# One kernel for two attention blocks: every engine's order and all PSUM banks dealt out anew

## The chip, the cores and the metric

The kernel runs on one core of a Trainium2 chip (trn2). The metric is the device time of one execution in microseconds, as the median of the runs shown. Engines are named as in the profile: PE (TensorE, matrix products), PEld (its weight loads), DVE (VectorE), ACT (ScalarE), POOL (GpSimd) and SP (SyncE, which here issues the DMAs).

## The reference, cut to what matters

The input is `x` and a context, both 64 sequences of 128 tokens with 256 features. Two layers follow one another.

```python
# layer 0: 16 heads of 64, keys and values from the context
qn, kn, vn = _ln(q), _ln(k), _ln(v)
attn = einsum('bhte,bhse->bhts', qn @ Wq, kn @ Wk) + rel_bias[idx]
out  = softmax(attn / 8) @ (vn @ Wv)
x    = q + out @ fc_w.T + fc_b
x    = x + gelu(_ln(x) @ W1.T + b1) @ W2.T + b2
# layer 1: 16 query heads of 16, one key/value head, a window of 128
scores = where(keep, (x @ Wq + bq) @ (ctx @ Wk + bk).T / 4, NEG)
attn = softmax(scores) @ (ctx @ Wv + bv) @ Wo + bo
gate = silu(concat([attn, x]) @ Wg + bg)
out  = attn * gate + x * (1 - gate)
y    = rms(out) * rms_w ; y = y - mean(y, axis=1)
```

## The kernel before, in words

Two sequences make a group `g`, so there are NG = 32 groups. The program of each engine is a straight list of calls that was written out by hand: a prologue, a loop `for r in range(3, NG - 3)` with 26 rounds, and an epilogue. In round `r` the attention of layer 0 for group `r` (with some of its fourth quarter from `r - 1`), the MLP of group `r - 1` and layer 1 of group `r - 2` run woven into each other. One round of the loop is called a pass here. Engines meet through counting semaphores: `till.wait_ge(name, count)` before a call, `.then_inc` at its end. The order in each list is the order of execution on that engine.

The attention of layer 0 goes in quarters `Q` of four heads: `proj_q`, `proj_k`, `proj_v` (dense products, three fp32r matmuls for one fp32 product), then `scores(g, Q)`, then `pv(g, Q)` (probabilities times V), then `fc` and `fc_lo`. Between `scores` and `pv`, DVE takes each of the two score banks with `min0` (bias and row minimum), ACT does `exps0`, DVE `inv0`, POOL `norm0`, DVE `turn0` (a transpose), and a DMA, `spread0`, lays it out. Layer 1 has `scores1(g, b)` and `pv1(g, b, n)` with `min1`, `exps1`, `inv1`, `norm1`, `turn1`, `spread1` in the same roles. `q_out` (ACT) and `k_out` (DVE) copy a projection out of PSUM into the single buffers `qT` and `kT`, so they wait until the scores of the quarter before are done, and the next scores wait for them.

Five kinds of product use a part of the PE array, that is, they are tiled: `scores` 64 rows by 128 columns (64\*128, line 757), `pv` 128\*64 (line 770), `scores1` 32\*128 (line 882), `pv1` and the small `kv_v` 128\*32 (lines 895 and 669). All others use 128\*128 and are called dense here. Two or four tiled matmuls that follow each other run on different parts of the array at once.

Every product writes one of eight PSUM banks; the tuple behind the bank in a call (`("min1", 8 * r - 7)`) is the copy that has to be done before the bank is written again. Before, banks 0 to 3 and 4 to 7 turn as two rings of four: `ring0[(r + i) % 4]`, `ring4[(r + i) % 4]`.

On ACT, `gelu` needs another table of functions than `exps0` and `exps1`; each change between them costs an `ACT_TABLE_LOAD`. Before, a pass runs both halves of `gelu` with no exponential between them.

## Time and profile before

| | us |
|---|---|
| three runs | 1902.6, 1903.36, 1907.44 |
| median | 1903.36 |
| profiled execution, span | 1903.7 |
| PE busy | 1840.5 (97% of the span) |
| PEld, DVE, ACT, POOL busy | 1696.0, 1518.9, 1538.4, 1294.2 |
| from one pass to the next | 56.74 |

The span is the profiled execution's own time from its first to its last instruction; it lies 0.3 us from the median of the runs. The page of the profile gives the busy time of each engine and the costliest groups of instructions; the time line gives instructions in order with their start; "..." stands where rows are left out. Matmuls are pipelined: one that is 0.28 us long starts 0.12 us after the one before it, so a start-to-start distance, not a duration, is what a matmul costs PE.

### The profile page before, as it was taken

Reading aid. Unit: us, or ns where it says so; the run is one execution under the profiler, and the core shown is the slowest. Engines: PE = TensorE matmul, PEld = TensorE weight load, DVE = VectorE, ACT = ScalarE, POOL = GpSimd, SP = SyncE. Lnnn points to the kernel's source line nnn. Section 1 sums busy time; section 2 is a strip of 40 time slices with the busy share of each in tenths; the row PEclk is TensorE's granted clock in tenths of the full one; section 3 lists DMA queues with packets and bytes.
Section 4 is the critical chain, followed back from the end, with each engine's and each line's share of the span. In section 5 each row is a group of like instructions: output and inputs, shape, how many; then the busy total and the mean of one; then the engine's idle time right before and its main releaser. Section 6 shows DMA issues by size and latency. Waiting matters only on the chain.

```text
span 1903.7 us, 55010 instructions
## 1 busy us (share of the span) xinstructions
PE 1840.5 (97%) x18660; PEld 1696.0 (89%) x18660; DVE 1518.9 (80%) x6787; ACT 1538.4 (81%) x5586; POOL 1294.2 (68%) x1328
## 2 busy tenths in 40 slices
...
GB/s 208 131 84 116 111 119 111 115 110 115 107 118 120 115 107 114 104 123 121 116 99 121 101 125 118 114 102 118 111 118 118 110 107 113 112 116 114 88 83 56
DMA packets 215273, 214.49 MB, mean 113 GB/s; under 512 B 29904, under 2 KB 197456, under 8 KB 214992
## 3 DMA queue, kind: packets, MB, share of 16 engines
...
q14 instruction: 133, 1.09, 0.2%
...
## 4 chain that ended last, share of the span: by engine, by line
PE 94%; DMA 2%; DVE 1%; ACT 1%; POOL 1%; issue 1%; SPq 0%; ACTq 0%; DVEq 0%; POOLq 0%
PE bank L576 12%; PE bank L577 11%; PE bank L578 11%; PE bank L594 8%; PE bank L590 8%; PE bank L591 8%; PE bank L757 7%; PE bank L770 7%; PE bank L582 4%; PE bank L882 4%; PE bank L895 3%; PE bank L583 3%; PE bank L586 3%; PE bank L654 2%; PE bank L600 2%
## 5 line engine op out<-in xcount | busy, mean ns | idle before, releaser
L2574 ACT ACTIVATE soft<-soft,row_min 128x128 f32<-128x128 f32 x1024 | 397.4, 393 | 16.3 <-DVE row_min L1728 16.0
L2494 ACT ACTIVATE soft<-soft,row_min 128x128 f32<-128x128 f32 x1024 | 397.8, 394 | 9.5 <-DVE row_min L1620 9.1
L235 DVE STREAM_TRANSPOSE turned<-soft 128x512 f32<-128x512 f32 x512 | 349.2, 692 | 9.7 <-POOL soft L3032 4.9
L3032 POOL TENSOR_TENSOR soft<-soft,inv_sum 128x512 f32<-128x512 f32 x256 | 267.1, 1044 | 127.3 <-DVE inv_sum L1628 123.3
L3041 POOL TENSOR_TENSOR soft<-soft,inv_sum 128x512 f32<-128x512 f32 x256 | 264.9, 1045 | 93.0 <-DVE inv_sum L1737 93.0
L1620 DVE CUSTOM_DVE_ANT_0 soft<-bank,relb 128x128 f32<-128x128 f32 x1024 | 231.6, 284 | 64.9 <-PE bank L757 64.5
L1728 DVE CUSTOM_DVE_ANT_0 soft<-bank,winb 128x128 f32<-128x128 f32 x1024 | 226.6, 284 | 16.9 <-PE bank L882 14.5
L2494 ACT ACTIVATION_READ_ACCUMULATOR soft<-soft,row_min 128x1 f32 x1024 | 196.7, 192 | 0.0
L2574 ACT ACTIVATION_READ_ACCUMULATOR soft<-soft,row_min 128x1 f32 x1024 | 195.1, 191 | 0.0
L1691 DVE TENSOR_TENSOR hidS<-hid,hidS 128x1024 fp32r<-128x1024 f32 x64 | 120.5, 1883 | 71.5 <-ACT hidS L2545 68.6
L757 PE MATMUL bank<-kT,qT 64*128 64x128 f32 x2048 | 148.7, 285 | 1.5 <-DVE kT L1600 1.4
L576 PE MATMUL bank<-wv,cT 128*128 128x256 f32 x512 | 147.2, 288 | 0.0
L770 PE MATMUL bank<-soft,V 128*64 128x128 f32 x2048 | 140.1, 279 | 3.7 <-issue 2.1
L577 PE MATMUL bank<-wv,cT 128*128 128x256 f32 x512 | 143.3, 280 | 0.0
L578 PE MATMUL bank<-wv,cT 128*128 128x256 f32 x512 | 143.1, 280 | 0.0
L757 PEld LDWEIGHTS bank<-kT,qT 64*128 64x128 f32 x2048 | 124.4, 187 | 20.7 <-issue 7.5
L1600 DVE TENSOR_SCALAR kT<-bank,bk 128x256 f32<-128x256 f32 x256 | 110.0, 471 | 39.7 <-PE bank L586 35.9
L770 PEld LDWEIGHTS bank<-soft,V 128*64 128x64 f32 x2048 | 109.4, 136 | 22.2 <-issue 5.7
L2526 ACT ACTIVATE hid<-bank,cols 128x256 f32<-128x256 f32 x256 | 106.2, 472 | 27.6 <-DVE hidS L1691 24.0
L590 PE MATMUL bank<-wfc,OT 128*128 128x256 f32 x512 | 127.8, 283 | 0.7 <-ACT OT L2505 0.6
L590 PE MATMUL bank<-w,hidS 128*128 128x256 f32 x512 | 123.5, 281 | 2.8 <-ACT hidS L2545 2.8
L591 PE MATMUL bank<-wfc,OT 128*128 128x256 f32 x512 | 126.0, 280 | 0.0
...
## 6 DMA issues: line engine op xcount, KB each, us to landing
soft<-turned SPq DMA_DIRECT2D x1024, 128.0 KB, 2.8
...
```

The source lines that it names most:

```text
L235: return eng.transpose(turned[:, slot, :, s % 2, :, :].rearrange("p j h b -> p h j b"), soft[:, s, :, :].rearrange("p h (j a) -> p h j a", ...
L576: pe.matmul(out, stat(LO), mov(HI), start=first, stop=False, **kw)
L577: pe.matmul(out, stat(HI), mov(LO), start=False, stop=False, **kw)
L578: return pe.matmul(out, stat(HI), mov(HI), start=False, stop=last, **kw)
L590: pe.matmul(out, stat(HI), mov(LO), start=first, stop=False, skip_group_check=True)
L591: return pe.matmul(out, stat(HI), mov(HI), start=False, stop=False, skip_group_check=True)
L757: last = pe.matmul(bank[i][:, h * SEQ:(h + 1) * SEQ], qT[half, c, b * SEQ:(b + 1) * SEQ], kT[half, c, b * SEQ:(b + 1) * SEQ], start=True, ...
L770: last = pe.matmul(bank[row:row + HS, col:col + SEQ], V[:, b, c * P + row:c * P + row + HS], pair_of_slots(Q % 2)[:, :, slot, h, :], start ...
L2494: last = act.activation(soft[:, s, h, :], soft[:, s, h, :], ACT.Exp, bias=row_min[:, s, h:h + 1], scale=-1.0, accum_out=row_sum[:, s, h:h ...
L2574: last = act.activation(soft[:, s, h, :], soft[:, s, h, :], ACT.Exp, bias=row_min[:, s, h:h + 1], scale=-1.0, accum_out=row_sum[:, s, h:h ...
L3032: pool.tensor_tensor(soft[:, m % NS0, :, :], soft[:, m % NS0, :, :], inv_sum[:, m % NS0, :].unsqueeze(2).broadcast_to([P, QUAD, SEQ]), ALU ...
L3041: pool.tensor_tensor(soft[:, s, :, :], soft[:, s, :, :], inv_sum[:, s, :].unsqueeze(2).broadcast_to([P, QUAD, SEQ]), ALU.mult).then_inc(se ...
```

## The change

No instruction's shape and no buffer changes. All five lists are in a new order, and the banks turn as two rings of three and one of two. In PE's loop, tiled products of both layers stand side by side in four stretches per pass, where there were eight. Inside the loop `proj_k`, `proj_q` and `scores` of the next group's first quarters are drawn forward, so that `scores(r + 1, 0)`, `pv(r, 3)` and `scores(r + 1, 1)` of the next round touch. On ACT, `exps0(r, 5)` now stands between the two halves of `gelu`. At the start, the DMAs of the weights and of `raw_x`, `raw_c` are issued in another order, and `cols_in` (which the first products and ACT's first weights wait for) comes seventh, not second.

PE's loop, tiled products and what stands next to them:

```diff
-        ring0 = banks[0:4]
-        ring4 = banks[4:8]
+        ring_a = [banks[i] for i in (0, 3, 6)]
+        ring_b = [banks[i] for i in (1, 5, 7)]
+        ring_c = [banks[i] for i in (2, 4)]
...
             for r in range(3, NG - 3):
...
-                scores(r, 0, (ring0[r % 4], ring4[r % 4]), (("v_out", 4 * r),), (("min1", 8 * r - 13),))
-                fc_lo(r - 1, 2, ring0[(r + 2) % 4])
...
-                scores(r, 1, (ring0[r % 4], ring4[r % 4]), (("min0", 8 * r + 1),), (("min0", 8 * r + 2),))
-                kv_k(r, ring4[(r + 2) % 4], ("q_out", 4 * r + 2))
...
-                pv1(r - 2, 0, 0, ring0[(r + 3) % 4], ("o_lo", 4 * r))
-                pv1(r - 2, 0, 1, ring0[(r + 3) % 4])
-                kv_v(r, ring4[(r + 2) % 4])
-                scores1(r - 2, 1, (ring4[r % 4], ring0[r % 4], ring0[(r + 1) % 4], ring4[(r + 3) % 4]), (("min0",
-                    8 * r + 4),), (("y_out", 2 * r - 4),), (("q_out", 4 * r + 3),), (("k_out", 4 * r + 3),))
-                out_mm(r - 2, 0, ring0[(r + 2) % 4], ("x1", r))
-                pv(r, 0, ring4[r % 4], ("min1", 8 * r - 11))
-                out_mm_lo(r - 2, 0, ring0[(r + 2) % 4])
...
-                scores(r, 2, (ring0[r % 4], ring0[(r + 1) % 4]), (("min1", 8 * r - 10),), (("min1", 8 * r - 9),))
-                turn_h(r - 1, ring0[(r + 3) % 4], ("v_out", 4 * r + 2))
...
-                pv(r, 1, ring0[r % 4], ("k_out", 4 * r + 4))
-                mlp_in(r - 1, 3, ring0[(r + 2) % 4], ("hid_out", 4 * r - 3))
...
-                scores(r, 3, (ring4[(r + 3) % 4], ring4[(r + 1) % 4]), (("q_out", 4 * r + 4),), (("hid_out",
-                    4 * r - 1),))
-                pv1(r - 2, 1, 0, ring0[(r + 2) % 4], ("hid_out", 4 * r))
-                pv1(r - 2, 1, 1, ring0[(r + 2) % 4])
-                proj_q(r + 1, 0, ring0[(r + 1) % 4], ("v_out", 4 * r + 3))
...
-                pv(r, 2, ring0[(r + 2) % 4], ("o1_lo", 2 * r - 2))
-                scores1(r - 1, 0, (ring4[(r + 3) % 4], ring0[r % 4], ring4[(r + 1) % 4], ring4[r % 4]), (("x2_lo",
-                    r),), (("o_lo", 4 * r + 2),), (("ag", 2 * r - 2),), (("q1_out", r),))
-                proj_v(r, 3, ring0[(r + 1) % 4], ("q_out", 4 * r + 5))
-                fc(r, 1, ring0[(r + 3) % 4])
-                proj_k(r + 1, 0, ring4[(r + 3) % 4], ("min1", 8 * r - 7))
...
-                pv(r, 3, ring0[r % 4], ("min1", 8 * r - 6))
...
+                scores(r, 1, (ring_c[r % 2], ring_b[(r + 1) % 3]), (("o_lo", 4 * r - 1),), (("q_out", 4 * r + 2),))
+                proj_v(r, 0, ring_b[(r + 2) % 3], ("k_out", 4 * r + 2))
...
+                center_out(r - 3, 1, ring_b[(r + 2) % 3], ("v_out", 4 * r + 1))
+                scores1(r - 2, 1, (ring_b[(r + 1) % 3], ring_c[(r + 1) % 2], ring_a[r % 3], ring_c[r % 2]), (("min0",
+                    8 * r + 4),), (("o_lo", 4 * r),), (("q_out", 4 * r + 3),), (("k_out", 4 * r + 3),))
+                pv1(r - 2, 0, 0, ring_b[r % 3], ("x1", r))
+                pv1(r - 2, 0, 1, ring_b[r % 3])
+                kv_v(r, ring_a[(r + 2) % 3])
+                pv(r, 0, ring_b[(r + 2) % 3], ("y_out", 2 * r - 4))
+                scores(r, 2, (ring_b[(r + 1) % 3], ring_b[r % 3]), (("min1", 8 * r - 11),), (("o1_lo", 2 * r - 3),))
+                out_mm(r - 2, 0, ring_c[(r + 1) % 2], ("min1", 8 * r - 10))
+                out_mm_lo(r - 2, 0, ring_c[(r + 1) % 2])
+                turn_h(r - 1, ring_b[(r + 1) % 3], ("min0", 8 * r + 5))
+                proj_k(r, 3, ring_a[r % 3], ("min1", 8 * r - 9))
+                proj_v(r, 1, ring_c[(r + 1) % 2], ("ag", 2 * r - 3))
+                mlp_in(r - 1, 0, ring_c[r % 2], ("min1", 8 * r - 8))
+                mlp_in_lo(r - 1, ring_c[r % 2])
+                mlp_in(r - 1, 1, ring_b[(r + 1) % 3], ("h_lo", r))
+                proj_q(r, 3, ring_a[(r + 1) % 3], ("kv_turn", r))
+                mlp_in(r - 1, 2, ring_c[r % 2], ("hid_out", 4 * r - 3))
+                proj_v(r, 2, ring_a[r % 3], ("k_out", 4 * r + 4))
+                fc(r, 0, ring_b[(r + 1) % 3], ("hid_out", 4 * r - 2))
+                mlp_out(r - 1, 0, 0, ring_c[(r + 1) % 2], ("v_out", 4 * r + 2))
...
+                scores(r, 3, (ring_b[(r + 2) % 3], ring_a[(r + 1) % 3]), (("o_lo", 4 * r + 1),), (("q_out",
+                    4 * r + 4),))
+                pv(r, 1, ring_c[r % 2], ("hid_out", 4 * r - 1))
+                pv1(r - 2, 1, 0, ring_b[r % 3], ("hid_out", 4 * r))
+                pv1(r - 2, 1, 1, ring_b[r % 3])
+                mlp_out_lo(r - 1, 0, 1, ring_c[(r + 1) % 2])
...
+                proj_v(r, 3, ring_c[r % 2], ("o_lo", 4 * r + 2))
+                proj_q1(r - 1, ring_a[(r + 1) % 3], ("y_out", 2 * r - 3))
+                proj_q1_lo(r - 1, ring_a[(r + 1) % 3])
+                pv(r, 2, ring_c[(r + 1) % 2], ("x2", r))
+                scores1(r - 1, 0, (ring_b[r % 3], ring_b[(r + 2) % 3], ring_a[r % 3], ring_a[(r + 1) % 3]), (("ag",
+                    2 * r - 2),), (("x2_lo", r),), (("v_out", 4 * r + 3),), (("q1_out", r),))
+                fc_lo(r, 1, ring_b[(r + 1) % 3])
+                proj_k(r + 1, 0, ring_c[r % 2], ("v_out", 4 * r + 4))
...
+                scores(r + 1, 0, (ring_a[r % 3], ring_a[(r + 1) % 3]), (("min1", 8 * r - 5),), (("min1", 8 * r - 4),))
+                pv(r, 3, ring_c[r % 2], ("k_out", 4 * r + 5))
```

ACT's loop, from `tanh` to the second half of the MLP:

```diff
                 tanh(r - 2, 0)
-                exps0(r, 5)
-                hid_out(r - 1, 0, ring0[(r + 2) % 4])
-                hid_out(r - 1, 1, ring0[(r + 1) % 4])
+                h_hi(r - 1, ring_b[(r + 1) % 3])
+                exps1(r - 2, 1, 2)
+                exps1(r - 2, 1, 3)
+                o_hi(r, 0, ring_b[(r + 2) % 3])
+                hid_out(r - 1, 0, ring_c[r % 2])
+                hid_out(r - 1, 1, ring_b[(r + 1) % 3])
+                v_out(r, 1, ring_c[(r + 1) % 2])
                 gelu(r - 1, 0)
                 hid_hi(r - 1, 0)
-                q_out(r, 3, ring4[(r + 3) % 4])
                 x_hi(r + 1)
-                hid_out(r - 1, 2, ring4[(r + 1) % 4])
+                exps0(r, 5)
                 square(r - 2, 0)
-                hid_out(r - 1, 3, ring0[(r + 2) % 4])
-                v_out(r, 2, ring0[(r + 1) % 4])
+                q_out(r, 3, ring_a[(r + 1) % 3])
+                hid_out(r - 1, 2, ring_c[r % 2])
+                hid_out(r - 1, 3, ring_b[r % 3])
                 gelu(r - 1, 1)
```

On PE, the place of the loop where the key product for layer 1, `kv_v`, stands, in the order before. `kT,qT` is `scores`, `soft,V` is `pv`, `soft,vpad` is `pv1`, `raw,wkv` is `kv_v`, `kpar,q1T` is `scores1`; `wog` and `wgx` are `out_mm`, and one row can stand for several instructions:

```order
L594 MATMUL bank<-wfc,OT 128x256 x4
L895 MATMUL bank<-soft,vpad 32x128 x16
L669 MATMUL bank<-raw,wkv 32x64 x8
L882 MATMUL bank<-kpar,q1T 128x256 x8
L590 MATMUL bank<-wog,o1T 128x512
...
L578 MATMUL bank<-wgx,x2T 128x256
L770 MATMUL bank<-soft,V 64x128 x8
L594 MATMUL bank<-wog,o1T 128x512 x2
...
L757 MATMUL bank<-kT,qT 128x128 x8
L600 MATMUL bank<-ident,normed 128x128 x4
```

The same place in the order after, and behind the dots the end of a round, where `scores(r + 1, 0)`, `pv(r, 3)` and the next round's `scores` meet:

```order
L935 MATMUL bank<-o1T,center 128x256
L883 MATMUL bank<-kpar,q1T 128x256 x8
L896 MATMUL bank<-soft,vpad 32x128 x16
L670 MATMUL bank<-raw,wkv 32x64 x8
L771 MATMUL bank<-soft,V 64x128 x8
L758 MATMUL bank<-kT,qT 128x128 x8
L591 MATMUL bank<-wog,o1T 128x512
```

```order
L758 MATMUL bank<-kT,qT 128x128 x8
L771 MATMUL bank<-soft,V 64x128 x8
L758 MATMUL bank<-kT,qT 128x128 x8
L577 MATMUL bank<-wv,cT 128x256
```

Three tiled stretches have become one, and the dense `out_mm` no longer lies between them; at the end of a round one `pv` is all that lies between two `scores`.

On ACT, around the first half of `gelu` (`hid<-hid`; `soft,row_sum` are the exponentials, `qT` is `q_out`, `hidS` `hid_hi`, `xT` `x_hi`), before:

```order
L2534 ACT_TABLE_LOAD
L2534 ACTIVATE hid<-hid 128x1024
L2545 CAST hidS<-hid 128x1024
L2476 ACTIVATE qT<-bank,bq 128x256 x2
L2455 CAST xT<-raw 128x512
L2526 ACTIVATE hid<-bank,cols 128x256 x2
L2604 ACTIVATE gate,sumsq<-ag 128x256
L2526 ACTIVATE hid<-bank,cols 128x256 x2
L2486 COPY V<-bank 128x512
L2534 ACTIVATE hid<-hid 128x1024
```

and after:

```order
L2527 ACT_TABLE_LOAD
L2527 ACTIVATE hid<-hid 128x1024
L2538 CAST hidS<-hid 128x1024
L2448 CAST xT<-raw 128x512
L2487 ACT_TABLE_LOAD
L2487 ACTIVATE soft,row_sum<-soft,row_min 128x128 x4
L2597 ACTIVATE gate,sumsq<-ag 128x256
L2469 ACTIVATE qT<-bank,bq 128x256 x2
L2519 ACTIVATE hid<-bank,cols 128x256 x4
L2527 ACT_TABLE_LOAD
L2527 ACTIVATE hid<-hid 128x1024
```

An exponential and with it two more table loads have moved between the halves, and `q_out(r, 3)` stands behind them. The whole program has 125 rows of table loads on ACT after, 65 before.

## Rows read from the trace of the kernel before

**Rows 1.** The page: the span and each engine's busy time.

```profile
span 1903.7 us, 55010 instructions
## 1 busy us (share of the span) xinstructions
PE 1840.5 (97%) x18660; PEld 1696.0 (89%) x18660; DVE 1518.9 (80%) x6787; ACT 1538.4 (81%) x5586; POOL 1294.2 (68%) x1328
```

**Rows 2.** Busy time by stretch: the loop's middle, the start, the end.

```profile
core 0: us, PE busy (x) PEld busy (x) DVE busy (x) ACT busy (x) POOL busy (x), PEclk, DMA share, GB/s
250.00:1700.00 1450.00, 1447.11 (x14848) 1343.71 (x14847) 1193.28 (x5390) 1215.15 (x4449) 1033.29 (x1049) 1.00 0.46 113
0.00:35.00 35.00, 14.22 (x104) 8.40 (x106) 18.65 (x35) 12.60 (x14) 10.23 (x24) 1.00 0.69 237
1830.00:1904.00 74.00, 40.04 (x356) 32.31 (x354) 37.85 (x164) 37.09 (x135) 37.64 (x43) 0.79 0.28 64
```

**Rows 3.** The chain that ended last, start, length: `scores1` of passes far apart.

```profile
286.67 1.15 PE bank L882 x16
...
1648.51 1.15 PE bank L882 x16
```

**Rows 4.** Time line of PE: dense, `pv`, `scores`, dense (start us, length us).

```profile
973.74 0.28 PE L590 MATMUL bank<-wfc,OT 128*128 128x256 f32 x1
...
973.86 0.28 PE L591 MATMUL bank<-wfc,OT 128*128 128x256 f32 x1
...
974.06 1.09 PE L770 MATMUL bank<-soft,V 128*64 128x128 f32 x16
...
975.09 1.16 PE L757 MATMUL bank<-kT,qT 64*128 64x128 f32 x16
...
976.18 0.74 PE L594 MATMUL bank<-wfc,OT 128*128 128x256 f32 x4
```

**Rows 5.** Time line of PE: `scores` to `turn_h`; then `scores`, `pv1`, dense.

```profile
939.45 0.66 PE L600 MATMUL bank<-ident,normed 128*128 128x128 f32 x4
...
955.03 1.16 PE L757 MATMUL bank<-kT,qT 64*128 64x128 f32 x16
...
956.12 1.08 PE L895 MATMUL bank<-soft,vpad 128*32 128x128 f32 x32
...
957.13 0.39 PE L582 MATMUL bank<-xT,wq 128*128 128x256 f32 x1
...
957.36 0.28 PE L583 MATMUL bank<-xT,wq 128*128 128x256 f32 x1
```

**Rows 6.** Each tiled line's matmuls: duration ns min/median/max, first and last start us.

```profile
L757 PE MATMUL bank<-kT,qT x2048: 272/272/374, 34.3 to 1805.4; 64*128 64x128 f32 x187
L770 PE MATMUL bank<-soft,V x2048: 272/273/324, 50.6 to 1826.3; 128*64 128x128 f32 x187
L882 PE MATMUL bank<-kpar,q1T x1024: 374/374/479, 117.9 to 1866.8; 32*128 32x256 f32 x171
```

**Rows 7.** Time line, `pv` before `scores1` and `proj_k` behind `fc`, PE and ACT.

```profile
966.23 1.09 PE L770 MATMUL bank<-soft,V 128*64 128x128 f32 x16
966.34 0.84 ACT L2564 ACTIVATE q1T<-bank,cols 128x256 f32<-128x256 f32 x2 [1.77 <-PE bank L586]
...
967.43 1.15 PE L882 MATMUL bank<-kpar,q1T 32*128 32x256 f32 x16
...
970.30 0.62 ACT L2464 CAST cT<-normed 128x512 fp32r<-128x512 f32 x1 [2.09 <-PE bank L578]
...
970.84 0.28 PE L591 MATMUL bank<-wfc,OT 128*128 128x256 f32 x1
...
971.07 0.36 PE L582 MATMUL bank<-cT,wk 128*128 128x256 f32 x1
...
971.26 0.28 PE L583 MATMUL bank<-cT,wk 128*128 128x256 f32 x1
```

**Rows 8.** Time line, `scores` to DVE's copy, and `k_out` to `scores`.

```profile
976.30 0.29 DVE L1620 CUSTOM_DVE_ANT_0 soft<-bank,relb 128x128 f32<-128x128 f32 x1 [0.19 <-PE bank L757]
...
977.15 0.71 DVE L235 STREAM_TRANSPOSE turned<-soft 128x512 f32<-128x512 f32 x1
...
38.52 0.88 DVE L1600 TENSOR_SCALAR kT<-bank,bk 128x256 f32<-128x256 f32 x2 [0.38 <-PE bank L578]
...
39.55 0.90 PE L757 MATMUL bank<-kT,qT 64*128 64x128 f32 x11 [0.49 <-DVE kT L1600]
```

**Rows 9.** Groups of ACT's instructions: table loads.

```profile
L2534 ACT ACT_TABLE_LOAD x32 | 41.1, 1283 | 0.6
L2494 ACT ACT_TABLE_LOAD x31 | 39.8, 1283 | 0.6
```

**Rows 10.** Time line of ACT: an exponential, then the first half of the MLP.

```profile
943.29 0.40 ACT L2494 ACTIVATE soft<-soft,row_min 128x128 f32<-128x128 f32 x1
943.58 0.20 ACT L2494 ACTIVATION_READ_ACCUMULATOR soft<-soft,row_min 128x1 f32 x1
943.68 0.40 ACT L2494 ACTIVATE soft<-soft,row_min 128x128 f32<-128x128 f32 x1
...
945.91 1.77 ACT L2526 ACTIVATE hid<-bank,cols 128x256 f32<-128x256 f32 x4
947.70 1.28 ACT L2534 ACT_TABLE_LOAD   x1
948.99 1.06 ACT L2534 ACTIVATE hid<-hid 128x1024 f32<-128x1024 f32 x1
950.08 1.05 ACT L2545 CAST hidS<-hid 128x1024 fp32r<-128x1024 f32 x1
```

**Rows 11.** Time line of the start: first copies, first dense product.

```profile
23.49 2.27 POOL L3049 TENSOR_TENSOR raw<-raw,tokens 128x512 f32<-128x512 f32 x1 [5.71 <-DMA raw<-in_x_t]
28.04 0.78 PE L582 MATMUL bank<-xT,wq 128*128 128x256 f32 x1
```

More of the change, by code:

```diff
@@ L987, in tensor_program @@
[L987 to L997 removed]
+            bias_mm(banks[1], SOFT0, 1, shifts[0], 0)
@@ new lines, in tensor_program @@
+            scores(2, 1, (banks[6], banks[4]), (("min0", 18),), (("q_out", 10),))
+            fc_lo(1, 3, banks[1])
+            proj_k(2, 2, banks[2], ("o_lo", 8))
+            proj_v(2, 0, banks[1], ("x1", 2))
+            scores1(0, 1, (banks[3], banks[6], banks[0], banks[7]), (("q_out", 11),), (("min0", 19),), (("min0",
+                17),), (("min1", 2),))
+            pv1(0, 0, 0, banks[1], ("v_out", 9))
+            pv1(0, 0, 1, banks[1])
+            proj_q(2, 3, banks[4], ("min0", 20))
@@ new lines, in tensor_program @@
+            proj_v(2, 1, banks[0], ("h_lo", 2))
+            proj_k(2, 3, banks[7], ("hid_out", 6))
+            proj_v(2, 2, banks[5], ("o_lo", 9))
+            mlp_out(1, 0, 0, banks[2], ("min0", 22))
+            mlp_out(1, 0, 1, banks[2])
+            mlp_in(1, 3, banks[0], ("v_out", 10))
+            pv(2, 1, banks[7], ("k_out", 12))
+            pv1(0, 1, 0, banks[6], ("ag", 1))
+            scores(2, 3, (banks[1], banks[0]), (("hid_out", 7),), (("hid_out", 8),))
+            proj_q(3, 0, banks[4], ("q_out", 12))
```

2259 lines of the change are left out of this document (1108 added, 1151 removed).

## The prediction

> **What bounds the kernel now.** I read the page's busy line first [rows 1]: PE is busy 97% of the span, the next engine 81%. A share is a mean, so the loop's middle by itself comes next [rows 2]: 1447.1 of 1450 us on PE (99.8%), at the full granted clock (1.00, the 2.4 GHz level), ACT 1215.2, DVE 1193.3. The chain that ended last passes `scores1` at 286.67 and 24 passes later at 1648.51 [rows 3], so a pass is (1648.51 - 286.67) / 24 = 56.74 us, and 26 passes are 1475 of 1903.7 us. In a pass ACT is busy 1215.15 / 1450 x 56.74 = 47.6 us, DVE 46.7. Every 0.1 us that PE loses or saves per pass is 2.6 us of the time, as long as PE stays full. But "busy" hides short stalls between products, so the rest is read from starts on the time line, not from busy time.
>
> **What a change of tiles costs.** Two dense products stand 0.12 us apart (973.74 and 973.86) [rows 4]. From the last dense one to `pv` it is 0.20: a gap of 0.08. `pv` takes 1.03 us until `scores` starts, `scores` 1.09 until the next dense product. Within both, a pair starts each 0.11 us, so eight pairs without any change would take 0.88; 0.15 and 0.20 are left, which is a gap of 0.09 to what follows plus a slower first product of 0.05 and 0.10. The first product's own length says the same [rows 6]: line 757 goes from 0.272 to 0.374, line 770 to 0.324, line 882 from 0.374 to 0.479. A dense product that comes first after tiled ones is 0.39 long where the others have 0.28, and the next one starts 0.23 later [rows 5]. `turn_h` in that place (0.66 for four, thus 0.33 for the first) pays only 0.05 [rows 5]. `scores` to `pv1` (955.03 to 956.12) costs what `scores` to dense does [rows 5]. So a change costs about 0.19 wherever two different tile shapes meet, also between two tiled kinds; a change to dense is not dearer than one to tiles.
>
> **Merging the stretches.** By the order a pass has 20 such changes before: 12 into a tiled kind and 8 into dense. After, it still has 12 into tiled kinds, but 4 into dense. The 12 stay because inside the new stretches the kinds differ. What goes is one change into dense per merge: 0.09 + 0.10 = 0.19 us; four are 0.76, less 0.04 because one of the dense ones was `turn_h`: **-0.72 us per pass**. Outside the loop the counts nearly cancel (4 more in the prologue, 2 fewer in the epilogue): 0. Four kinds of change in the new order don't occur before: `scores` to `pv` (twice), `scores1` to `pv1`, `kv_v` to `pv`, `pv` to `pv1`. From below, they could be free (another -0.67 per pass); from above, one could cost twice what the seen ones do (+0.2 each). I take the seen value, since the two tile-to-tile changes that the trace has, `pv` to `scores` and `scores` to `pv1`, both show it [rows 4, 5].
>
> The Trainium skill, "TensorEngine Tiling (Array Packing)", section "Tiling Modes", says that changing the mode, not just the tile, drains TensorE. It would put the unseen changes at the seen price, as I did, and count changes rather than stretches. A count by stretches would give 8 x 0.19 = 1.5 us per pass instead of 0.72.
>
> **Waits that go or stay.** `scores1(r - 1, 0)` behind `pv(r, 2)` waits for ACT's copy of `q1T`: `pv` at 966.23 + 0.82 is at its last pair, and `scores1` starts at 967.43, 0.38 after it and not 0.20 [rows 7]. The new order keeps the same neighbours (`proj_q1_lo`, `pv`, `scores1`), so 0.18 stays. `proj_k` for the next group waits behind `fc` for `c_hi`, which ACT starts at 970.30: the gaps are 0.23 and 0.19 and not 0.12 [rows 7], 0.18 too much. `c_hi` waits for `proj_v(r, 3)` (its row says 2.09 us idle for PE). `proj_v(r, 3)` moves ahead of `proj_q1`, `pv` and `scores1`, more than 3 us earlier, so this stall goes: **-0.18**. Next late there is nothing that I find.
>
> **Waits that come.** Now `scores(r, 1)` has only `pv(r - 1, 3)` between itself and `scores(r, 0)`. `kT` and `qT` are single buffers, so their copies start when `scores(r, 0)` is done. A copy starts 0.32 us after the last `scores` product has started (976.18 - 0.20 to 976.30), `kT` takes 0.88 and `scores` starts 0.15 behind it (38.52 + 0.88 to 39.55) [rows 8]: 1.35. Through ACT it is 0.32 + 0.84, and 0.25 until PE starts (966.34 to 967.43) [rows 7]: 1.41. Between them PE has 0.20 + 1.03 = 1.23. So 0.12 to 0.18, **+0.16** per pass; 0.1 if both copies start at once, 0.25 if DVE is within a 0.29 us `min0` step [rows 8] then. `exps0(r, 5)` between the halves of `gelu` brings ACT two more table loads per pass, 1.28 each [rows 9]. From the end of `hid_out` (945.91 + 1.77) to `gelu` at 948.99 there is nothing else than the load [rows 10], so 2 x 1.283 = 2.57, and ACT's work is 47.6 + 2.6 = 50.1 of some 56.1 us. The list from the first `gelu`'s load to `q_out(r, 3)` is now 1.28 + 1.06 + 1.05 (`hid_hi`) + 0.62 (`x_hi`, as `c_hi`) + 1.28 + 4 x 0.39 (`exps0`, from 943.29 to 943.68) + 0.42 (`square`) = 7.3 us without a pause [rows 7, 10]. Set on PE's clock, `hid_hi` of either half ends 0.2 to 0.3 us before `mlp_out` wants it and `q_out(r, 3)` ends between 0 and 0.1 after PE is at `scores(r, 3)`. From below these cost nothing; from above each of three is 0.2 late, 0.6. I take **+0.15**, since the slack that I work out is at its edge, not beyond it. `o1_hi` to `scores(r, 2)`, `min1` to `out_mm`, and `k_out(r + 1, 0)` to `scores(r + 1, 0)` have 0 to 0.3 us left by the same count and are put at nothing: what covers them is the dense products ahead of them.
>
> The Trainium skill, "ScalarE: Activation LUTs", section "What ACT_TABLE_LOAD costs", gives about 1283 ns for the load and about 1380 ns more for a drain, 2.66 us for each switch. The load's length is the trace's; the drain is not seen in it, since `gelu` starts where the load ends and `hid_out` ends where it begins [rows 10]. By the page ACT would have 5.3 us more per pass instead of 2.6, and the chain to `q_out` would be late by more than a microsecond.
>
> **The start.** PE has 14.2 us of work in the first 35 [rows 2]. POOL starts on `raw` at 23.49 after 5.71 us of waiting for the DMA of `raw_x`, and the first long dense run begins at 28.04 [rows 11]. The new order issues `raw_x` earlier, but `cols_in`, for which ACT's first weights wait, later. The gain can be at most what PE waits there, and part is given back: bounds -3 and +4, I take **-1**. At the end (1830 to 1904) PE is busy 40 of 74 us at a mean granted clock of 0.79 [rows 2], part of it at the lower level; the order there is new too, but the chain through both layers for the last groups is as long: 0, with 2 us either way.
>
> **The sum.** Per pass -0.72 - 0.18 + 0.16 + 0.15 = -0.59; 26 passes: -15.3; with the start -16.3. The profiled execution has 1903.7, so its like is 1887.4; the median lies 0.3 below that: **1887 us**.
>
> **The rivals.**
> A, the forecast, with its small terms at their bounds (the unseen changes at a little less or more, waits at 0 to 0.3 per pass): 1880 to 1894. Chance 0.50.
> B, tile changes inside a stretch are cheaper than between dense and tiled, or the copies start in time. For it: `pv` first costs only 0.05, and `kv_v` follows `pv1` without a change of shape. Against: the two seen tile-to-tile changes are at full price. All four kinds free: 1887 - 26 x 0.67 = 1870. Only no new waits: 1887 - 26 x 0.31 = 1879. Chance 0.20.
> C, the banks become the bound: products of a stretch now end in a burst, four to five banks at once, with rings of three and two instead of four. Each bank comes free only after its copy, `min0` taking 0.85 us per bank (976.30 to 977.15) [rows 8]. Against: DVE has 10 us idle per pass. With another +0.3 to +0.75 per pass: 1895 to 1906. Chance 0.19. This is also the case in which the merge is made but buys nothing measurable.
> The Trainium skill has this in "TensorEngine Tiling (Array Packing)", section "Performance Considerations", under PSUM bottleneck: tiling speeds up the products but not the evacuation of PSUM.
> D, slower: ACT becomes the bound in the stretch around `exps0(r, 5)`. It has 56.7 - 47.6 = 9.2 us idle per pass now. With 50.1 of work a pass of 56.7 leaves 6.6; if waits that can't be moved (for a bank, for DVE's maxima) take more than that, ACT sets the pass. That is the point from which it decides. At 7.5 us of such waits a pass is 57.6: 1903.4 + 26 x 0.9 = 1927. For it: the ACT list is strict, and two 1.28 us blocks lie where `q_out` is needed. Against: 84% busy with idle spread over the pass. Chance 0.11.
> That the change doesn't do what it says is out: the order shows four tiled stretches per pass.
>
> **How the numbers follow.** A measurement here can tell about 0.3%, 5.7 us: faster is below 1897.7, slower above 1909.1. Faster is A, B and a little over half of C: 0.80. Same is the rest of C and a mild D: 0.09. Slower is the rest of D and a start or end that goes badly: 0.11. The range reaches from half-way into B's cheapest, 1868, over A, to most of C, 1902; above it lies D with the end of C.
>
> **What would show it.** In the profile after: passes of `scores1` 56.15 us apart; four tiled stretches with first products still at 0.374, 0.324 and 0.479, and 0.20 from one kind to the next; `proj_k` behind `fc_lo` at 0.12 spacing; `scores(r, 1)` starting 1.4 us after the last product of `scores(r, 0)`, released by `kT` or `qT`; 62 or so more table loads on ACT (125 rows against 65) and ACT busy 50 per pass. Wrong it would be if PE's rows show idle time before `mlp_out`, `scores(r, 3)` or `out_mm` of more than 0.3 us, released by ACT, or if `scores` and `pv` next to each other overlap. If the pass has saved 0.6 and the time has not, look at the start.

## The result

| | before | after |
|---|---|---|
| median of 20 runs, us | 1904.15 (1901.52 to 1907.44) | 1909.1 (1904.03 to 1912.53) |
| ratio after / before | | 1.0027, interval 1.002 to 1.0034 |
| span of the profiled execution, us | 1903.7 | 1905.6 |

The changed kernel is no faster: 0.27% slower, which is clear of the scatter of the runs but, by the prediction's bound of 0.3%, a "same" on its slow side. The forecast was 1887, with 1868 to 1902 as its range. Of the ten runs of e5_var_later, told below, one took 6099 us and is left out of its ratio.

The page of the changed kernel, the busy line, and the stretches that stand in [rows 2] for the kernel before (lengths, then busy time of PE, PEld, DVE, ACT and POOL):

```profile
span 1905.6 us, 55062 instructions
## 1 busy us (share of the span) xinstructions
PE 1831.2 (96%) x18660; PEld 1692.2 (89%) x18660; DVE 1467.7 (77%) x6787; ACT 1618.5 (85%) x5646; POOL 1307.0 (69%) x1328
```

```profile
250.00:1700.00 1450.00, 1435.66 (x14819) 1335.61 (x14810) 1143.65 (x5380) 1281.08 (x4481) 1042.26 (x1048) 1.00 0.45 113
0.00:35.00 35.00, 17.05 (x133) 12.39 (x134) 17.17 (x43) 12.76 (x16) 7.86 (x24) 1.00 0.66 230
1830.00:1906.00 76.00, 43.18 (x368) 34.88 (x366) 38.81 (x157) 37.89 (x136) 37.80 (x43) 0.76 0.27 63
```

PE has the same 18660 products and is busy 9.3 us less in the whole, 11.5 us less in the loop's middle. Against [rows 1, 2] that looks like a gain, but it is the idle time that has grown: 14.3 of 1450 us and not 2.9. Where PE waits in this stretch, by the view of waits (in total, times, longest), is for the kernel before one row and after three:

```profile
PE bank L582 <- DVE row_min L1728: 0.2, 1, 0.2
```

```profile
PE bank L758 <- DVE kT L1593: 5.7, 11, 0.8
PE bank L771 <- DMA soft<-turned: 3.5, 7, 1.4
PE bank L758 <- ACT qT L2469: 0.4, 1, 0.4
```

This view lists only waits long enough to leave PE idle. The short ones hide in "busy" and show in the starts. So I took, for the last 24 passes of the loop in each kernel, the start-to-start distance at every place of the pass, and took off what the same pair of products has where nothing is late. The mean pass is 56.74 us before and 56.80 after (two `scores1` of the changed kernel that stand 23 passes apart start at 343.65 and 1649.81, which gives 56.79), and it divides so:

```profile
343.65 1.15 PE L883 MATMUL bank<-kpar,q1T 32*128 32x256 f32 x16
...
1649.81 1.15 PE L883 MATMUL bank<-kpar,q1T 32*128 32x256 f32 x16
```

| us per pass | before | after | difference |
|---|---|---|---|
| gaps at changes of tile | 1.86 (20 changes) | 1.50 (16) | -0.36 |
| slower first dense products | 0.79 | 0.42 | -0.37 |
| waits between products of different calls | 0.38 | 1.14 | +0.76 |
| from the first to the last start of a tiled call | | | 0 |
| the rest | | | +0.03 |
| pass | 56.74 | 56.80 | +0.06 |

The merge pays what was worked out for it, 0.73 us. No tiled call has become longer in itself (`scores` takes 0.89 us from its first start to its last in both kernels, `pv` 0.82, `scores1` 0.77). Waits take it all back:

| where PE waits, us per pass | before | after |
|---|---|---|
| `scores(r, 1)`, behind `pv(r - 1, 3)` | 0 | 0.37 (at least 0.19) |
| `out_mm(r - 2, 1)`, with its slower first product | 0 | 0.36 |
| `pv(r, 0)`, after behind `kv_v` | 0.01 | 0.18 (0 to 1.48) |
| `scores(r, 2)`, `turn_h`, `scores(r, 3)` | 0 | 0.07, 0.09, 0.05 |
| `scores1(r - 1, 0)` | 0.18 | 0.02 |
| `proj_k(r + 1, 0)` behind `fc` | 0.19 | 0 |

The mean hides two kinds of pass. Of the 24 before, 22 are 56.70 to 56.80 us long. Of the 24 after, 12 are 56.51 to 56.54, which is 0.2 shorter, and the other 12 are 56.76 to 58.03. In 11 of these 12 `scores(r, 1)` is over its least, by 0.25 to 0.73, and in 3 `pv(r, 0)` waits 0.58 us or more. Below that a wait of `pv(r, 0)` costs nothing: in the short passes it is up to 0.25, and where it is, `scores(r, 2)` and `turn_h` wait 0.1 less each. So the change does gain, in the half of the passes in which no copy and no DMA is much too late.

The spans of the two profiled executions differ by 1.9 us, the medians by 5. The table of places explains the 1.9 and not the other 3. A span is 1.7 us shorter than the time of the same run (1905.6 against 1907.3 for the profiled run after); by this the profiled execution lies 1.8 us under its median after and, if the same holds, about 1.3 over it before.

**The tiled products after.** The time line of PE where three stretches became one, the counterpart of [rows 4, 5]:

```profile
930.07 0.28 PE L935 MATMUL bank<-o1T,center 128*128 128x256 f32 x1
930.27 1.15 PE L883 MATMUL bank<-kpar,q1T 32*128 32x256 f32 x16
931.35 1.08 PE L896 MATMUL bank<-soft,vpad 128*32 128x128 f32 x32
932.25 0.41 PE L670 MATMUL bank<-raw,wkv 128*32 128x64 f32 x16
932.59 1.09 PE L771 MATMUL bank<-soft,V 128*64 128x128 f32 x16
933.72 1.16 PE L758 MATMUL bank<-kT,qT 64*128 64x128 f32 x16
934.81 0.50 PE L591 MATMUL bank<-wog,o1T 128*128 128x512 f32 x1
```

From `scores1` to `pv1` it is 1.08 (0.77 of its own and 0.30 to what follows, as to a dense product before), from `scores` to dense 1.09, as in [rows 4]. The mean gaps over the passes say it more sharply: `scores` to `pv` 0.202, `pv` to `pv1` 0.202, `scores1` to `pv1` 0.304, `kv_v` to `pv` 0.149 where nothing waits; before, `scores` to dense has 0.202, `scores1` to dense 0.304, `kv_v` to `scores1` 0.149. The unseen kinds of change cost what the seen ones do. The Trainium skill, "TensorEngine Tiling (Array Packing)", section "Tiling Modes", says that changing the mode drains TensorE; with these gaps the trace agrees, also between two tiled kinds.

**`scores(r, 1)`.** The end of a pass, PE, ACT and DVE; first a pass with the least wait, then the one with the longest of the 24:

```profile
918.47 1.16 PE L758 MATMUL bank<-kT,qT 64*128 64x128 f32 x16
...
919.56 1.09 PE L771 MATMUL bank<-soft,V 128*64 128x128 f32 x16
...
919.74 0.84 ACT L2469 ACTIVATE qT<-bank,bq 128x256 f32<-128x256 f32 x2 [0.42 <-PE bank L758]
919.75 0.88 DVE L1593 TENSOR_SCALAR kT<-bank,bk 128x256 f32<-128x256 f32 x2 [0.22 <-PE bank L758]
...
920.78 0.49 PE L758 MATMUL bank<-kT,qT 64*128 64x128 f32 x4
```

```profile
406.05 1.28 POOL L3097 TENSOR_TENSOR x<-x,rows 128x512 f32<-128x512 f32 x1 [0.44 <-DMA x<-in_x]
406.14 1.22 DVE L1504 TENSOR_SCALAR stat<-stat 128x2 f32<-128x2 f32 x1
...
406.50 1.16 PE L758 MATMUL bank<-kT,qT 64*128 64x128 f32 x16
...
407.59 1.09 PE L771 MATMUL bank<-soft,V 128*64 128x128 f32 x16
...
407.77 0.84 ACT L2469 ACTIVATE qT<-bank,bq 128x256 f32<-128x256 f32 x2 [0.42 <-PE bank L758]
...
408.55 0.84 DVE L1593 TENSOR_SCALAR kT<-bank,bk 128x256 f32<-128x256 f32 x2
...
409.53 0.72 PE L758 MATMUL bank<-kT,qT 64*128 64x128 f32 x8 [0.85 <-DVE kT L1593]
```

Above, both copies start as soon as `scores(r, 0)` is done, and `scores(r, 1)` comes 1.22 behind `pv` where 1.03 would be free of waits: the 0.19 of the forecast. Below, `kT` starts 0.78 later than `qT`, and DVE has just had a 128x2 instruction, `var_x`, that took 1.22 us, with its list to catch up. That the one comes from the other is what e5 tests.

**`out_mm(r - 2, 1)`.** PE, ACT and DVE there:

```profile
961.45 0.35 ACT L2580 CAST o1T<-bank 128x256 fp32r<-128x256 f32 x1
...
961.84 0.42 DVE L1745 TENSOR_TENSOR o1T<-bank,o1T 128x256 fp32r<-128x256 f32 x1
...
962.32 0.19 PEld L591 LDWEIGHTS bank<-wog,o1T 128*128 128x128 f32 x1 [0.29 <-DVE o1T L1745]
962.32 0.50 PE L591 MATMUL bank<-wog,o1T 128*128 128x512 f32 x1
...
962.66 0.40 PE L592 MATMUL bank<-wog,o1T 128*128 128x512 f32 x1
```

The product reads only ACT's half, `o1_hi`, done at 961.80. It waits for DVE's `o1_lo`, done at 962.26, since in the new deal it writes the bank that `pv1` wrote (`ring_b[r % 3]`, drained by `("o1_lo", 2 * r - 2)`). Before, it wrote `ring4[(r + 1) % 4]`, drained by `("min0", 8 * r + 8)`.

### The profile page after: what moved, and what is told of

It reads as the page before. It is cut to its first block, busy times and chain, and to the rows that moved or that the text cites. A ratio compares the mean times of both kernels' runs of the same rounds, so it can differ in the third digit from the quotient of the medians.

```text
span 1905.6 us, 55062 instructions
## 1 busy us (share of the span) xinstructions
PE 1831.2 (96%) x18660; PEld 1692.2 (89%) x18660; DVE 1467.7 (77%) x6787; ACT 1618.5 (85%) x5646; POOL 1307.0 (69%) x1328
## 3 DMA queue, kind: packets, MB, share of 16 engines
q14 instruction: 133, 1.09, 0.2%
## 4 chain that ended last, share of the span: by engine, by line
PE 55%; ACT 22%; DVE 7%; issue 7%; SPq 3%; DMA 3%; POOL 1%; ACTq 0%; DVEq 0%; POOLq 0%
PE bank L577 7%; PE bank L578 7%; PE bank L579 7%; PE bank L758 4%; ACT soft L2487 4%; PE bank L591 4%; PE bank L771 4%; PE bank L595 4%; ACT L2487 4%; PE bank L592 3%; ACT hid L2519 3%; SPq L246 3%; PE bank L883 3%; ACT hid L2527 3%; PE bank L583 2%
## 5 line engine op out<-in xcount | busy, mean ns | idle before, releaser
L236 DVE STREAM_TRANSPOSE turned<-soft 128x512 f32<-128x512 f32 x512 | 356.3, 698 | 31.8 <-POOL soft L3034 13.7
L3025 POOL TENSOR_TENSOR soft<-soft,inv_sum 128x512 f32<-128x512 f32 x256 | 284.9, 1113 | 125.9 <-DVE inv_sum L1621 124.9
L3034 POOL TENSOR_TENSOR soft<-soft,inv_sum 128x512 f32<-128x512 f32 x256 | 265.6, 1044 | 104.3 <-DVE inv_sum L1730 104.0
L591 PE MATMUL bank<-w,hidS 128*128 128x256 f32 x512 | 124.7, 280 | 2.7 <-ACT hidS L2538 2.7
L592 PE MATMUL bank<-w,hidS 128*128 128x256 f32 x512 | 123.9, 279 | 0.0
L2469 ACT ACTIVATE qT<-bank,bq 128x256 f32<-128x256 f32 x256 | 106.5, 467 | 17.6 <-PE bank L758 17.2
L3139 POOL TENSOR_TENSOR o1T<-ag,o1T 128x256 fp32r<-128x256 f32 x63 | 69.1, 1096 | 75.0 <-ACT o1T L2603 68.5
```

Source lines behind the costliest of these rows:

```text
L236: return eng.transpose(turned[:, slot, :, s % 2, :, :].rearrange("p j h b -> p h j b"), soft[:, s, :, :].rearrange("p h (j a) -> p h j a", ...
L591: pe.matmul(out, stat(HI), mov(LO), start=first, stop=False, skip_group_check=True)
L592: return pe.matmul(out, stat(HI), mov(HI), start=False, stop=False, skip_group_check=True)
L3025: pool.tensor_tensor(soft[:, m % NS0, :, :], soft[:, m % NS0, :, :], inv_sum[:, m % NS0, :].unsqueeze(2).broadcast_to([P, QUAD, SEQ]), ALU ...
L3034: pool.tensor_tensor(soft[:, s, :, :], soft[:, s, :, :], inv_sum[:, s, :].unsqueeze(2).broadcast_to([P, QUAD, SEQ]), ALU.mult).then_inc(se ...
```

## The experiments

Two theories from here. **Theory 1**: merging is worth its 0.73 us, and single late operands, banks and DMAs take it back, each for a reason of its own. **Theory 2**: ACT, with two more table loads per pass, sets the pass, and whatever is mended at one place returns at the next. Times are compared with the changed kernel's 1909.1 by each run's ratio to the kernel before. The pass is the mean over the last 24 passes of the loop in one profiled execution each; before it is 56.74.

| kernel | median us | ratio to before, interval | pass us |
|---|---|---|---|
| changed kernel | 1909.1 | 1.0027, 1.002 to 1.0034 | 56.80 |
| e1_o1_first | 1936.59 | 1.0167, 1.0152 to 1.0182 | 57.85 |
| e2_k_first | 1907.89 | 1.0017, 1.0008 to 1.0027 | 56.77 |
| e3_one_table | 1897.85 | 0.9963, 0.995 to 0.9976 | 56.48 |
| e4_split | 1909.34 | 1.0019, 1.0009 to 1.0028 | 56.83 |
| e5_var_later | 1907.41 | 1.002, 1.001 to 1.003 | 56.76 |
| e6_center_first | 1897.66 | 0.9969, 0.996 to 0.9979 | 56.37 |
| e7_one_merge (on before) | 1936.75 | 1.0179, 1.0162 to 1.0196 | 58.00 |
| e8_wrap_split | 1907.11 | 1.0011, 1.0002 to 1.0021 | 56.77 |
| e9_both | 1897.31 | 0.9961, 0.9948 to 0.9973 | 56.31 |
| e10_before_one_table (on before) | 1905.05 | 1.0004, 0.9995 to 1.0013 | 56.76 |

### Does ACT set the pass? (e3, e10)

```diff
-                act.activation(flat(hid[:]), flat(hid[:]), ACT.Gelu)
+                act.activation(flat(hid[:]), flat(hid[:]), ACT.Tanh)
```

> The changed kernel with the function of gelu replaced by Tanh, which the exponentials' table has: the MLP's activation is not the reference's, and the four table loads per pass go (125 to a few in all), 5.1 us of ACT's work per pass. Nothing is moved. Theory 1 (waits at places where a copy, a bank or a DMA is late; ACT's load counts only in the 0.045 before scores(r, 3) and in part of the 0.3 at out_mm(r - 2, 1), behind a load): the time falls by 3 to 12 us, to 1897 to 1906. Theory 2 (ACT sets the pass): it falls by 0.6 us per pass or more, 16 us, to 1893 or less, and all waits of PE for ACT vanish.

This kernel leaves gelu out and is there for its time alone; one table load is left of 125. Measured: 1897.85, 11 to 12 us less than the changed kernel, 0.33 per pass. ACT's busy time in the loop's middle fell from 1281 to 1157 us, 4.9 us per pass, for a gain of a fifteenth of that:

```profile
250.00:1700.00 1450.00, 1435.62 (x14900) 1341.83 (x14896) 1174.36 (x5392) 1156.66 (x4398) 1041.39 (x1052) 1.00 0.46 114
```

By places, nearly all of it is one: `out_mm(r - 2, 1)` no longer waits (0.36), since the load at the head of `exps0(r, 6)` stood ahead of `o1_hi` on ACT. The 0.05 at `scores(r, 3)` went too; the waits at `scores(r, 1)` (0.44) and `pv(r, 0)` (0.20) grew. So theory 2 falls: ACT is not the bound. But ACT's load does count at one place of the changed kernel. Is that so in the kernel before as well?

> The kernel before with the function of gelu replaced by Tanh, as in e3_one_table for the changed one: the MLP's activation is not the reference's, and the two table loads per pass go, 2.6 us of ACT's work. In the changed kernel this took 11 us off, 0.34 per pass at out_mm(r - 2, 1). If that gain came from the loads that the change adds or moved out_mm behind: here little, 0 to 3 us less, 1901 to 1904. If any relief of ACT gives the same in either kernel: 8 us or more less, 1896 or below.

Measured: ratio 1.0004, no change. So in the kernel before no table load costs PE anything that the time shows; in the changed one they cost it at `out_mm`, and a little at `scores(r, 3)`.

### The wait at `out_mm` (e1, e6)

```diff
                 o_hi(r, 1, ring_c[r % 2])
+                o1_hi(r - 2, 1, ring_b[r % 3])
                 exps0(r, 6)
-                o1_hi(r - 2, 1, ring_b[r % 3])
...
+                o1_lo(r - 2, 1, ring_b[r % 3])
                 inv0(r, 6)
-                o1_lo(r - 2, 1, ring_b[r % 3])
```

> The changed kernel, with ACT's o1_hi(r - 2, 1) ahead of exps0(r, 6) and DVE's o1_lo ahead of inv0(r, 6) in the loop. In the changed kernel out_mm(r - 2, 1) writes the bank that pv1 wrote and so waits for o1_lo: its gap is 0.36 us and not 0.12 and the next one is 0.10 longer, 0.34 per pass. Theory 1 (merging pays its full 0.72 us per pass, and waits at four or five places take it back): this place falls to 0.12, the pass by 0.3, the time by about 8 us: 1901 where the changed kernel has 1909, ratio to the kernel before 0.998. Theory 2 (ACT, with its two more table loads, sets the pass, so that a wait taken away at one place comes back at the next): the time stays within 2 us of 1909, and other waits on PE grow by 0.3 per pass.

Measured: 1936.59, 27 us more than the changed kernel; neither theory had that. The wait before `out_mm` went as wanted, but a new one of 1.50 us stands before `turn_x2` (the pass grows by 1.05 only, since `out_mm` and `scores(r, 1)` wait less). ACT's rows, and PE's `turn_x2`:

```profile
974.61 0.37 ACT L2580 CAST o1T<-bank 128x256 fp32r<-128x256 f32 x1 [1.86 <-PE bank L935]
975.00 1.28 ACT L2487 ACT_TABLE_LOAD   x1
```

```profile
979.83 0.41 PE L601 MATMUL bank<-ident,x 128*128 128x128 f32 x2 [1.34 <-DVE x L1693]
```

`o1_hi` writes a buffer that `center_out(r - 2, 0)` (line 935) still reads. I had counted only its input. ACT's list is strict, so ACT stood still for 1.86 us, with `exps0(r, 6)` behind it. DVE's `inv0(r, 6)` waits for that one, and behind `inv0` in DVE's list stands `x2_sum`, on which `turn_x2` depends. A wait is not moved by moving the waiting instruction. So the whole chain has to come forward, on ACT, POOL and PE in this order:

```diff
+                x_hat_hi(r - 2, 0)
                 gelu(r - 1, 1)
                 hid_hi(r - 1, 1)
-                x_hat_hi(r - 2, 0)
...
+                x_hat_lo(r - 2, 0)
                 x1_b2(r - 1)
-                x_hat_lo(r - 2, 0)
...
+                center_out(r - 2, 0, ring_a[(r + 1) % 3], ("min0", 8 * r + 8))
                 mlp_out(r - 1, 1, 0, ring_c[(r + 1) % 2])
                 mlp_out(r - 1, 1, 1, ring_c[(r + 1) % 2])
-                center_out(r - 2, 0, ring_a[(r + 1) % 3], ("min0", 8 * r + 8))
```

To these come the two edits of e1_o1_first.

> The changed kernel with the whole chain to o1_hi(r - 2, 1) drawn forward, not its end alone: x_hat_hi ahead of the second gelu on ACT, x_hat_lo ahead of x1_b2 on POOL, center_out ahead of mlp_out(r - 1, 1, 0) on PE, o1_hi ahead of exps0(r, 6) on ACT, o1_lo ahead of inv0(r, 6) on DVE. Theory 1 (the 30 us that the first such edit lost came from ACT standing behind center_out for 1.9 us): out_mm(r - 2, 1) starts without a wait (0.12, and 0.24 to the next product), turn_x2 too; mlp_out(r - 1, 1, 0) waits up to 0.1; the pass falls by 0.25 to 0.34, the time by 7 to 9 us to 1901, ratio 0.9985. Theory 2 (ACT has no room: each instruction put forward delays another on PE's path as much): 1909 or more.

Measured: 1897.66, 0.58% under the changed kernel and 0.31% under the kernel before. The pass is 0.44 shorter, more than the 0.34 that theory 1 allowed. The place itself gives 0.36: the shortest passes fell from 56.51 to 56.15. The rest comes mostly from `scores(r, 1)` and `pv(r, 0)`, which waited 0.09 and 0.08 less, with `var_x` over 1 us long in 3 passes only; no part of the edit was made for that. PE, ACT and DVE at the place:

```profile
955.94 0.37 ACT L2580 CAST o1T<-bank 128x256 fp32r<-128x256 f32 x1
...
956.60 0.42 DVE L1745 TENSOR_TENSOR o1T<-bank,o1T 128x256 fp32r<-128x256 f32 x1
...
959.45 0.39 PE L591 MATMUL bank<-wog,o1T 128*128 128x512 f32 x1
...
959.68 0.39 PE L592 MATMUL bank<-wog,o1T 128*128 128x512 f32 x1
```

`o1_lo` is done 2.4 us before PE wants it, and the first product of `out_mm` is 0.39 us long and not 0.50. `mlp_out(r - 1, 1, 0)`, which I had put at up to 0.1 late, doesn't wait. ACT has the same work per pass as in the changed kernel (1289 us of 1450, over shorter passes), which is theory 2's second refutation: with its load unchanged, another order was enough.

### The wait before `scores(r, 1)` (e2, e5, e8)

```diff
                 o_lo(r - 1, 2, ring_c[r % 2])
-                inv1(r - 2, 0, 2)
                 k_out(r, 1, ring_b[(r + 2) % 3])
+                inv1(r - 2, 0, 2)
```

> The changed kernel, with k_out(r, 1) ahead of inv1(r - 2, 0, 2) in DVE's loop, nothing else. At the end of a pass scores(r, 1) starts 0.57 us behind pv(r - 1, 3) in the mean, 0.39 at the least, where 0.20 is free of waits. Theory 1a (the mean lies over the least because inv1 stands ahead of k_out and waits for an exponential): the mean falls to 0.39 to 0.42, 0.15 per pass, about 4 us: 1905, ratio 1.0007. Theory 1b (the excess comes from DVE being late for another reason, as a small copy that takes 1.2 us while POOL works): the mean stays over 0.5, and the time within 2 us of 1909. In both the least stays 0.39, since the copy of kT or qT takes longer than one pv.

Measured: the mean gap is 0.59 (0.57 in the changed kernel), and the interval of the time overlaps the changed kernel's. `inv1` is not what `k_out` is late for; theory 1b holds. The view of the single line then gives the suspect, min, median and maximum of its duration in the changed kernel:

```profile
L1504 DVE TENSOR_SCALAR stat<-stat x32: 133/165/1218, 6.4 to 1721.9; 128x2 f32<-128x2 f32 x32
```

```diff
                 min0(r, 0, ring_a[(r + 2) % 3])
+                var_x(r + 1)
...
-                var_x(r + 2)
                 turn1(r - 1, 0, 0)
```

> The changed kernel with one small DVE instruction moved: var_x, 128x2, from the end of a pass to behind min0(r, 0) of the next. In the passes where scores(r, 1) is later than its least (0.39 us), the trace shows this instruction 0.9 to 1.2 us long where it has 0.16 otherwise, while POOL's x_fcb (1.28 us) runs, and k_out behind it late. Theory A (that hold-up is the reason): the mean gap from pv(r - 1, 3) to scores(r, 1) falls from 0.57 to 0.42 or less, in nearly all passes 0.39; 0.15 us per pass, 4 us: 1905, ratio 1.0005. Theory B (DVE is late there for all it has to do): the mean stays over 0.52 and the time at 1909.

Measured: the gap is 0.39 in 23 of 24 passes, as theory A says; 0.17 per pass is gone at this place. But the time is 1907.41, by the ratios 1.3 us less and not 4, which the intervals don't tell from nothing, and the pass is 0.05 shorter. Waits on PE in the loop's middle:

```profile
PE bank L771 <- DMA soft<-turned: 6.8, 12, 1.7
PE bank L758 <- DVE kT L1593: 0.5, 1, 0.5
PE bank L758 <- ACT qT L2469: 0.4, 1, 0.4
```

Set beside the three rows of the changed kernel above: `kT` fell from 5.7 to 0.5 us, and the DMA of `spread0` rose from 3.5 to 6.8. `pv(r, 0)` waits 0.33 per pass and not 0.18. At its new place `var_x` is held again, for 0.3 to 1.0 us in 14 of 32 cases, and there it stands ahead of the chain to `pv(r, 0)`. Here something did return at the next place, but by way of DVE, not of ACT.

The least 0.19 needs dense work between the two `scores`:

```diff
+                fc_lo(r - 1, 2, ring_b[r % 3])
                 scores(r, 1, (ring_c[r % 2], ring_b[(r + 1) % 3]), (("o_lo", 4 * r - 1),), (("q_out", 4 * r + 2),))
                 proj_v(r, 0, ring_b[(r + 2) % 3], ("k_out", 4 * r + 2))
                 kv_k(r, ring_a[(r + 2) % 3], ("min0", 8 * r + 1))
-                fc_lo(r - 1, 2, ring_b[r % 3])
```

> The changed kernel with one merge undone where it costs a wait: fc_lo(r - 1, 2), four dense products of 0.47 us, stands between pv(r - 1, 3) and scores(r, 1), and no longer behind kv_k. The change into dense costs 0.195 again, the wait of 0.37 in the mean (0.19 at the least) goes nearly whole. Theory 1: the pass falls by 0.1 to 0.18, the time by 2.5 to 4.5 us, to 1905 to 1906.5, ratio 1.001. If merging were a gain here: the time rises by up to 5 us.

Measured: the wait falls from 0.37 to 0.04, the change costs 0.195 again, and `pv(r, 0)` waits 0.31 and not 0.18; 0.03 per pass is left of the 0.1 to 0.18. The time is 1907.11, whose interval overlaps the changed kernel's. So this merge bought nothing that shows: a copy chain of 1.41 us does not fit behind one `pv` of 1.03 plus its change. Why `pv(r, 0)` waits longer here was not looked into.

### One merge alone, one merge undone (e7, e4)

```diff
-                out_mm(r - 2, 0, ring0[(r + 2) % 4], ("x1", r))
                 pv(r, 0, ring4[r % 4], ("min1", 8 * r - 11))
+                out_mm(r - 2, 0, ring0[(r + 2) % 4], ("x1", r))
```

> The kernel before with one merge alone: pv(r, 0) ahead of out_mm(r - 2, 0), so that pv1, kv_v, scores1 and pv touch. One change into dense less. By the price of a merge alone: 0.19 per pass, 4.9 us less, 1899. By the DMA: pv(r, 0) stands 0.13 to 1.26 us behind the last landing of spread0(r, 0) in the kernel before and is drawn forward by 1.75 us, so it waits 0.65 us in most passes and up to 1.75; mean 1.0, less the 0.19: 0.8 per pass, 21 us more, 1925, ratio 1.011.

Measured: 1936.75, 33 us more. The change count fell to 19 and its price with it (0.195, gaps and first products), and `pv(r, 0)` waits 1.40 us in the mean. The direction was that of the DMA's theory, the size was not, and the rows show why. Waits on PE in the loop's middle, and one pass of each kind:

```profile
PE bank L770 <- DMA soft<-turned: 19.8, 12, 2.1
PE bank L770 <- DVE row_min L1728: 13.7, 13, 1.1
```

```profile
948.23 1.09 PE L770 MATMUL bank<-soft,V 128*64 128x128 f32 x16 [1.05 <-DVE row_min L1728]
...
1006.73 1.97 PE L770 MATMUL bank<-soft,V 128*64 128x128 f32 x16 [1.93 <-DMA soft<-turned]
```

In 11 of 24 passes the DMA is last, but in all of them the bank is late: `pv(r, 0)` writes the bank that `scores1` just before it has filled (`ring4[r % 4]`, `("min1", 8 * r - 11)`), so it waits at least 1.12 us for `min1`. With the banks as they were, this merge is not to be had. The changed kernel gives `pv(r, 0)` a bank that `y_out` sets free (`("y_out", 2 * r - 4)`); the run doesn't tell more about why the change deals all banks anew.

```diff
                 pv(r, 1, ring_c[r % 2], ("hid_out", 4 * r - 1))
+                mlp_out_lo(r - 1, 0, 1, ring_c[(r + 1) % 2])
                 pv1(r - 2, 1, 0, ring_b[r % 3], ("hid_out", 4 * r))
                 pv1(r - 2, 1, 1, ring_b[r % 3])
-                mlp_out_lo(r - 1, 0, 1, ring_c[(r + 1) % 2])
```

> The changed kernel with one of its tiled stretches cut in two: mlp_out_lo(r - 1, 0, 1), four dense products, stands between pv(r, 1) and pv1(r - 2, 1, 0) instead of behind pv1. Five stretches per pass, one change into dense more. The price of a merge, 0.09 for the gap and 0.10 for the slower first dense product, says: the pass grows by 0.19, the time by 4.9 us, to 1914, ratio 1.0053. If merging were worth nothing (the drain hidden or the same wherever the tiles change), it stays at 1909.

Measured: 1909.34, as the changed kernel. Yet merging is not worth nothing: the gaps grew by 0.09 and the first dense products by 0.105, as expected. The first wait before `out_mm(r - 2, 1)` fell from 0.26 to 0.06 at the same time, because PE came there 0.195 later. Work put in ahead of a wait is free as long as the wait lasts; the total alone would have misled.

### Both repairs together (e9)

The edits of e6_center_first, and `var_x(r + 1)` behind `turn0(r, 1)`, past both chains.

> The changed kernel with the chain to o1_hi drawn forward as in e6_center_first, and var_x behind turn0(r, 1) of the next pass, where neither k_out nor spread0(r, 0) waits for it. If the two places are apart: scores(r, 1) 0.39 behind pv in nearly all passes (0.47 in the mean in e6_center_first), spread0(r, 0) no later, the pass 0.05 to 0.1 shorter, the time 1 to 3 us less than e6_center_first, 1895 to 1897, ratio to the kernel before 0.9955 to 0.9965. If what DVE is held up by only moves on: the wait before pv(r, 0) grows by as much, as it did with var_x behind min0(r, 0), and the time stays at 1897.7 or above.

Measured: 1897.31, ratio 0.9961; e6_center_first has 0.9969, so the two can't be told apart by time. The gap before `scores(r, 1)` is 0.39 in 23 of 24 passes. The wait for `kT` is down to 0.5 us in the loop's middle, the DMA's is 3.4, as in the changed kernel. But in e6_center_first they are 2.5 and 1.5, and set against that kernel `scores(r, 1)` gained 0.07 per pass while `pv(r, 0)` went from 0.10 to 0.18. `var_x` is not what holds `pv(r, 0)` here, since it is 0.13 us long in all but one pass. So whether the two places are apart stays open: the pass is 0.06 shorter in one execution of each, and the DMA's lateness differs from execution to execution. Both kernels are 0.3 to 0.4% faster than the kernel before and 0.6 to 0.7% faster than the changed one.

## Why the prediction was wrong

- **What bounds the kernel**: right. PE is the bound before and after, and short stalls had to be read from starts.
- **The price of a change and the merges**: right. 20 changes became 16, and -0.73 per pass was measured against -0.72. The unseen kinds cost what the seen ones do. The rival B is out.
- **Waits that go**: `proj_k` behind `fc` lost its 0.18 (0.19 measured). `scores1(r - 1, 0)`, said to stay at 0.18, fell to 0.02. Its copy ends at the same distance from the start of `pv` in both kernels (0.95), but PE starts 0.10 behind it after and 0.25 before; what else `scores1` waited for before was not found. This error helped the forecast.
- **Waits that come**: here the prediction failed, by size and by count. It put them at +0.31 per pass; they are 1.11. By its terms:
  - `scores(r, 1)`: +0.16 forecast, 0.19 at the least as worked out, but 0.37 in the mean. The step took both copies as ready to start. DVE, held up by `var_x`, is not in 11 of 24 passes. In the kernel before this instruction takes 0.34 us at the most, so its own row gave no warning; `hid_lo` did (last section), but I bounded the term by one `min0` step of 0.29.
  - `exps0(r, 5)` and ACT's chain: +0.15 forecast for three places. `scores(r, 3)` waits 0.05, `mlp_out` not at all. The ACT load that does cost, in front of `exps0(r, 6)`, stands at a place that this step didn't look at.
  - `out_mm(r - 2, 1)`: forecast nothing, 0.36 measured, the largest single miss. The step "put at nothing: what covers them is the dense products ahead of them" has `min1` as what `out_mm` waits for. That is the tuple of `out_mm(r - 2, 0)`; the one of `out_mm(r - 2, 1)`, which leads through its new bank to `o1_lo` and from there to `o1_hi` behind a table load, was not followed.
  - `pv(r, 0)`: not in the sum at all, 0.18 measured. The merge pulls it 4 us nearer to `scores1(r - 1, 0)` (20.5 and not 24.6 us behind it). The trace of before shows it 1.1 to 1.3 us behind the last landing of its DMA in 11 of 24 passes and right behind it, at 0.14, in 5; I never set that distance against the move.
  - `scores(r, 2)`, `turn_h`: 0.16 together, for banks that were written a few products earlier. This is rival C's mechanism, smaller than C had it. The 0.36 of `out_mm` is a wait for a bank too, but e6_center_first takes it away with the same banks, so it is one late chain and not the bound that C has.
- **The sum**: per pass -0.59 forecast, +0.06 measured. With the terms as measured the same sum gives -0.73 for the merges, -0.35 for the waits that go, +1.11 for those that come and a rest of +0.03.
- **Start and end**: -1 forecast for the start. The first `scores1` begins at 118.3 and not at 117.9 [rows 6], so it is +0.4: PE waits 10.2 us for `cols_in` there. The end moved by 0.1.
- **The chances**: C (0.19) was the nearest, but at 1909 the time lies beyond its 1906, and most of what was lost went by single late chains. The outcome, a same, had 0.09. D, ACT as the bound, is refuted by e3_one_table and e6_center_first: 4.9 us less work on ACT gave 0.33, nearly all of it at one place.
